# A gated recurrence on one Trainium2 core: the reset product's whole value on GpSimd, and the state's own candidate term as early products on TensorE

## The reference, cut to what matters

```python
def step(h, inp):
    x_t, prop = inp
    comb = jnp.concatenate([x_t, h], axis=-1)
    z = jax.nn.sigmoid(comb @ Wz + bz)
    r = jax.nn.sigmoid(comb @ Wr + br)
    comb2 = jnp.concatenate([x_t, r * h], axis=-1)
    h_cand = jnp.tanh(comb2 @ Wh + bh)
    h_new = (1.0 - z) * h + z * h_cand
    h_next = jnp.where(prop, jnp.tanh(h_new @ Wp + bp), h_new)
    return (h_next, h_new)
```

## Time and profile before

| what | us |
|---|---|
| median of 3 runs | 2821.99 (2821.02 to 2822.12) |
| the profiled execution | 2822.85 |
| its span, first to last instruction | 2821.1 |
| TensorE busy | 2596.0, 92% |
| VectorE busy | 1630.2, 58% |
| ScalarE busy | 1037.0, 37% |
| GpSimd busy | 413.3, 15% |
| mean granted TensorE clock | 0.981 of full speed |

### The profile page before, as it was taken

The page is one execution under the profiler, slowest core; times in us unless marked ns, Lnnn a source line. Parts: engine busy times, 40 slices in busy tenths (PEclk is TensorE's granted clock), DMA queues, the critical chain, the costliest instruction groups (busy, mean ns, idle before and its releaser), DMA issues.

```text
span 2821.1 us, 76597 instructions
## 1 busy us (share of the span) xinstructions
PE 2596.0 (92%) x29142; PEld 1991.4 (71%) x29142; DVE 1630.2 (58%) x7909; ACT 1037.0 (37%) x3200; POOL 413.3 (15%) x481
## 2 busy tenths in 40 slices
PE   7999999999999999988999998999988999999897
PEld 5777777777777777777888886556873334387586
DVE  4666666766666666665555554665433666742722
ACT  2223333333322222225666663112543232443622
POOL 1001000000000000001111111223440000001433
PEclk9999999999999999999999998999998999989999
DMA  9925454221120100006777776222443331000123
GB/s 308 323 89 205 159 176 161 70 70 61 60 89 11 40 11 6 11 10 214 257 250 259 251 255 203 83 76 79 140 139 135 124 112 62 1 0 0 50 88 105
DMA packets 173633, 334.36 MB, mean 119 GB/s; under 512 B 33400, under 2 KB 104672, under 8 KB 161952
## 3 DMA queue, kind: packets, MB, share of 16 engines
q1 hardware_dynamic: 154080, 279.78, 29.8%
q0 software_dynamic: 17344, 48.78, 4.8%
q10 hardware_dynamic: 1920, 1.84, 0.2%
HBM read 186.50 MB, written 143.85 MB: 117 GB/s over the span
## 4 chain that ended last, share of the span: by engine, by line
PE 81%; DVE 8%; ACT 5%; issue 3%; DMA 2%; POOL 0%; SPq 0%; POOLq 0%; DVEq 0%; ACTq 0%
PE bank L1805 21%; PE bank L1792 9%; PE bank L1970 7%; PE bank L1981 7%; PE bank L2076 4%; DVE rhpart L1255 3%; ACT gate_r L801 3%; PE bank L2177 3%; PE bank L2221 3%; PE bank L2293 3%; PE bank L2127 2%; PE bank L2138 2%; PE bank L2384 2%; PE bank L2396 2%; PE bank L2085 2%
## 5 line engine op out<-in xcount | busy, mean ns | idle before, releaser
L1805 PE MATMUL bank<-h_high,WB 128*128 128x8 f16 x9216 | 418.9, 169 | 32.3 <-DVE h_high L1271 28.7
L1805 PEld LDWEIGHTS bank<-h_high,WB 128*128 128x128 f16 x9216 | 339.2, 105 | 135.1 <-DVE h_high L1271 83.4
L1805 PE MATMUL bank<-rhpart,WB 128*128 128x8 f16 x6144 | 290.1, 171 | 84.7 <-DVE rhpart L1255 84.4
L1805 PEld LDWEIGHTS bank<-rhpart,WB 128*128 128x128 f16 x6144 | 243.9, 106 | 130.9 <-DVE rhpart L1255 127.8
L1805 PE MATMUL bank<-h_low,WB 128*128 128x8 f16 x4608 | 299.4, 171 | 0.2
L1792 PE MATMUL bank<-XT,WB 128*128 128x128 f32 x768 | 295.5, 482 | 0.0
L1970 PE MATMUL bank<-WA,WB 128*128 128x256 f16 x1872 | 256.3, 274 | 3.3 <-DMA b_up<-b_cols 3.3
L1981 PE MATMUL bank<-WB,hid 128*128 128x256 f16 x1872 | 254.9, 273 | 0.0
L801 ACT ACTIVATE gate_r<-bank 128x16 f32<-128x16 f32 x512 | 93.7, 183 | 435.0 <-PE bank L1805 435.0
L1365 DVE SCALAR_TENSOR_TENSOR hid<-WA,hid 128x256 f16<-128x256 f32 x312 | 132.0, 423 | 187.4 <-ACT hid L859 187.4
L1805 PEld LDWEIGHTS bank<-h_low,WB 128*128 128x128 f16 x4608 | 213.2, 106 | 12.4
(11 more groups left out here) (367 smaller groups left out, 4434.5 us busy)
## 6 DMA issues: line engine op xcount, KB each, us to landing
WB<-w_parts SPq DMA_DIRECT2D x78, 1024.0 KB, 5.2
tile_rows<-WA SPq DMA_DIRECT2D x32, 2176.0 KB, 20.8
WA<-tile_rows SPq DMA_DIRECT2D x78, 272.0 KB, 2.9
WB<-in_L_ffn_w SPq DMA_DIRECT2D x32, 512.0 KB, 5.1
w_parts<-WB SPq DMA_DIRECT2D x32, 512.0 KB, 3.2
GB<-gates SPq DMA_DIRECT2D x8, 2048.0 KB
WA<-expert_rows SPq DMA_DIRECT2D x16, 512.0 KB, 5.9
WB<-expert_rows SPq DMA_DIRECT2D x16, 512.0 KB, 8.6
```

Source lines behind the costliest of these rows:

```text
L1805: last = nc.tensor.matmul(bank[:, m * width + s * B:m * width + (s + 1) * B], wpart[:, g, w, k, m * P:(m + 1) * P], part[a][:, k * B:(k + ...
```

## The change

The sum (gate_r + 1) x h is taken apart. The candidate's own term of `h` becomes twelve products of the state's parts, on TensorE, straight after the update gate's and without a wait. `rhpart` is then made of gate_r x h alone: VectorE makes the high part, GpSimd makes the whole product `rfull` from the same two operands in a new function `reset_product`, and VectorE's low part waits for both. On GpSimd the scatters are sent one at a time at fixed steps of a turn (`SEND_AT`; in the three turns from turn 5 on, `CATCH_UP_AT`), behind that step's `reset_product`, where two or more stood in a row before. The wait for `xg_zeroed` stands in front of turn 5's first `reset_product`.

```diff
-            def scatter_block(b):
+            def scatter_side(b, c):
                 q = b % GRING
                 pool.wait_ge(slots_ready, b + 1)
                 pool.wait_ge(row_ready, b + 1)
-                for c in range(2):
-                    nc.gpsimd.indirect_dma_start(xg[0], bass.IndirectOffsetOnAxis(ap=slots[:, c, b:b + 1], axis=0),
-                                                 row_out0[:, q, c], None).then_inc(moved[q], 16)
+                nc.gpsimd.indirect_dma_start(xg[0], bass.IndirectOffsetOnAxis(ap=slots[:, c, b:b + 1], axis=0),
+                                             row_out0[:, q, c], None).then_inc(moved[q], 16)
+
+            def reset_product(it, s):
+                n = it * STEPS + s
+                h = entry_s[:] if s % CHUNK == 0 else odd(hist[:, s - 1])
+                pool.wait_ge(r_ready, n + 1)
+                nc.gpsimd.tensor_tensor(rfull[:], gate_r[:], h, ALU.mult).then_inc(rh_full, 1)
...
+            SEND_AT = {3: (0, 0), 11: (0, 1)}
+            CATCH_UP_AT = {3: (-1, 0), 5: (-1, 1), 11: (0, 0), 13: (0, 1)}
+            LATE = 2
+            FIRST = GRING + 1
             for it in range(TURNS):
-                if it == GRING + 1:
+                if it == FIRST:
                     pool.wait_ge(xg_zeroed[0], ZEROED[0])
-                    for b in range(GRING - 1):
-                        scatter_block(b)
-                if it > GRING:
-                    scatter_block(it - 2)
-                for half in range(2):
-                    history(it, half)
-            for b in range(TURNS - 2, NBLK):
-                scatter_block(b)
+                for s in range(STEPS):
+                    reset_product(it, s)
+                    if FIRST <= it < FIRST + 3:
+                        back_by, c = CATCH_UP_AT.get(s, (0, None))
+                        if c is not None:
+                            scatter_side(2 * (it - FIRST) + 1 + back_by, c)
+                    elif it >= FIRST + 3:
+                        _, c = SEND_AT.get(s, (0, None))
+                        if c is not None:
+                            scatter_side(it - LATE, c)
+                    if s % (STEPS // 2) == STEPS // 2 - 1:
+                        history(it, s // (STEPS // 2))
+            for b in range(TURNS - LATE, NBLK):
+                for c in range(2):
+                    scatter_side(b, c)
...
                     dve.wait_ge(r_ready, n + 1)
-                    nc.vector.scalar_tensor_tensor(rhpart[:, 0], gate_r[:], 1.0, h, ALU.add, ALU.mult).then_inc(rh_part, 1)
-                    nc.vector.scalar_tensor_tensor(rfull[:], gate_r[:], 1.0, h, ALU.add, ALU.mult).then_inc(rh_full, 1)
+                    nc.vector.tensor_tensor(rhpart[:, 0], gate_r[:], h, ALU.mult).then_inc(rh_part, 1)
+                    dve.wait_ge(rh_part, 2 * n + 1)
                     dve.wait_ge(rh_full, n + 1)
                     nc.vector.tensor_tensor(rhpart[:, 1], rfull[:], rhpart[:, 0], ALU.subtract).then_inc(rh_part, 1)
...
                     recur(gates[1], 1, W, s, h_parts, None).then_inc(z_psum, 1)
+                    recur(gates[2], 2, W, s, h_parts, None)
                     recur(gates[2], 2, W, s, rh_parts, lambda a: pe.wait_ge(rh_part, n * 2 + a + 1)).then_inc(c_psum, 1)
```

## The result

The changed kernel takes 2869.4 us (median of 4 runs, 2868.0 to 2871.1), the kernel before 2822.1 us (4 runs, 2821.0 to 2822.3): 1.017 times as long, 95% interval 1.0157 to 1.0182. The change costs 47 us. The forecast was 2862 us in a range of 2805 to 2935, slower with a chance of 0.75.

What follows compares the result with a forecast made beforehand. The chain of waits between engines was taken to bound the recurrence, with the low part releasing the candidate. The longer GpSimd path adds 512 x 0.078 = 40 us to 2822.85, other parts nothing: 2862 us, range 2805 to 2935.

Steps and rivals of the forecast that it cites:

- The low part releases the candidate: End of TensorE's candidate group: the low part, not the high one, releases it; a later low part costs its full delay.
- The path through GpSimd: From the reset gate's tanh to VectorE's low part: 0.405 us against 0.327, so 0.078 us a step, 40 us.
- The 16-column product: GpSimd's whole product: 225 ns, extrapolated from 459 ns on 128 columns and 1260 on 512.
- the iota's 143 ns: Lower bound for GpSimd's product, from an iota of 17 columns.
- The early products "at nothing": TensorE before the wait for `rhpart`: twelve products a step take 0.315 us, costed at nothing.
- The cover: TensorE's 0.33 us hole before the candidate, and behind it 0.09 us in which the low part is still out.
- The later `keep`, `mix_times` and `mix_plus`: VectorE operations queued behind the wait for GpSimd: 0.26 us of cover stays before ScalarE's candidate, costed at nothing.
- the scatters spread over the turn: GpSimd's scatters, one a place, later by at most half a turn; costed at nothing.
- the wait for the zeroed rows: GpSimd at turn 5: rows already zeroed when the product comes at about 231; otherwise about 4.3 us, once.
- Faster: Rival: GpSimd's fixed part is shorter, path 0.253 us with the lower ends, 2794 us; chance 0.15.
- Held by VectorE's reads: Rival: GpSimd's product waits until VectorE's ends, 0.208 us a step, 107 us in all, 2929 us; chance 0.13.
- TensorE becomes the bound: Rival: early products at 0.055 us each end the high parts 0.24 us over today's, 2945 us; chance 0.02.

Runs made afterwards that it cites:

- the first profile: The profile of the changed kernel, against the kernel before; its profiled execution took 2867.96 us.
- the second: The changed kernel measured once more, nothing altered: 2869.9 us, 1.0172 times the kernel before.
- the first run: The kernel before with the twelve early products and plain products, the whole one still on VectorE: 2832.5 us, 1.0046 times the kernel before.
- the kernel with the shared product: The changed kernel with GpSimd making 8 of the whole product's 16 columns and VectorE the other 8: 2871.4 us, 1.0180 times the kernel before.

## Why the prediction was right, and where it was off

**The low part releases the candidate.** This was read from a group of loads 0.09 us longer than its twin, and it held. Leaving the low part out takes 0.19 us off every step, the sum of that wait and four products, in two kernels.

**The path through GpSimd.** Forecast 0.08 + 0.225 + 0.10 = 0.405 us. Measured over the 158 steps between 400 and 800 us: 0.079 to GpSimd's start and 0.323 from there to the low part, 0.402 in all, against 0.328 in the kernel before; the product itself takes 0.220. The 16-column product was extrapolated from two much wider ones, and that was right to 5 ns. The other bound, the iota's 143 ns, was far off. This term was sized at 512 x 0.078 = 40 us; the steps paid 0.068 in the first profile and 0.073 in the second, 35 to 37 us.

**The early products "at nothing".** This is the step of the prediction that failed, by a small amount. The cover was what it was said to be: within the steps the products cost 0.0002 us. What I had not seen is that the cover is a stretch of time on TensorE and not a supply of instructions. Alone they cost 14 us against the kernel before, 10.9 of it in gaps; in the changed kernel about 7. This is nearly the whole difference between 40 forecast and 47 measured: 35 for the steps, 7 for TensorE's gaps, 3 for VectorE's late starts, 45 in the profiled execution. That the sum came so near is in part luck: the 10 us that the forecast did not have are set off by some 4 that its step had too much.

**Costed at nothing and right.** The later `keep`, `mix_times` and `mix_plus`, the scatters spread over the turn, and the wait for the zeroed rows, which the slower steps had overtaken by turn 5.

**The rivals.** "Faster" fell with the product's 0.220 us. "Held by VectorE's reads" had 0.13 and 2929 us: GpSimd's product takes 211 to 223 ns beside VectorE's read and 212 to 224 alone, and VectorE's second product is not held by GpSimd's either. The rule that the Trainium skill states in "SBUF — State Buffer", section "Who interferes with whom", did not show at this size; a hold of some ten nanoseconds would be below what these rows tell. The section names the hold for the whole instruction in its line on VectorE's two-port modes; for two SBUF inputs it says that they contend, and not for how long. "TensorE becomes the bound" fell with the first run: the group starts when it did.

## What to carry to other kernels

Look inside the group that ends a step: if it lasts longer than a twin of the same size, a second, later operand may be what releases it, and that operand's path is then the one to shorten. An operation moved to an idle engine pays for two hand-overs, here 0.08 us there and 0.10 back around 0.22 of work, against 0.09 us for one more operation in the queue where it stood; that was a loss of 0.07 us a step, though GpSimd was busy for 15% of the span and VectorE for 58%. And work that fits into a hole on the clock can still cost a little: here the hole was also time in which TensorE's next block of instructions arrived.

## What the runs showed of the hardware that was not expected

- TensorE's stream of small products (128 x 8, each with its own weight load) runs with hardly a gap at 16 products a microsecond, and at 21 and more shows gaps of up to 1.8 us in the middle of a group; they come to 7 to 16 us in some 1200. They end at one place in every 256 of its instructions (16 KB), 1.2 to 2.0 us after the end of a packet on the instruction queue.
- In 15 steps of 512, the same ones in the changed kernel and in the one without early products, VectorE paused for 0.30 to 0.37 us in front of the 64th of 128 of its records, four times in front of the low part and eleven times in front of `keep` or `mix_times`. In the kernel with the shared product, whose programs are laid out differently, other steps stand out. What it waits for is open.
- Halving a 16-column product on GpSimd saved 0.02 us of its 0.22 and brought the waiting engine forward by nothing.
